# Grouping the split-array matmuls of a fused attention and mixture-of-experts kernel into two bursts a pass

## The chip, the cores and the metric

The kernel runs on one core of one Trainium2 chip, as one program. The metric is the device time of one execution in microseconds (us). Before the change it is 1570.88 us, the median of three runs (1569.62 to 1571.24).

## What is computed

`x` is 64 sequences of 128 tokens by 256, `ctx` 64 by 128 by 192, all float32. In the reference, cut to what matters:

```python
q = (layernorm(x) @ w_q) ; k = ctx @ w_k ; v = ctx @ w_v        # 16 heads of 64
attn = softmax(q k^T / 8) ; x = x + (attn v) @ w_o + b_o         # per sequence
h = layernorm(x)
g = top 2 of softmax(h @ gate) over 8 experts, renormalised
x = x + sum_e g_e * (relu(h @ W1[e] + b1[e]) @ W2[e] + b2[e])     # 256 -> 512 -> 256
```

## The kernel before

The first part, some 1,090 of the 1,568 us, is the attention: 32 passes over pairs of sequences (256 tokens), written as one loop body that each engine runs in its own order (`body(it)` of TensorE, VectorE, ScalarE, GpSimd and the DMA queue of SyncE), with the passes -1, 0, 1 and 31 unrolled. The second part multiplies the tokens, sorted by expert, in tiles of 256.

Each pass has eight slots, n = 0 to 7. What the slots hold is written out by hand:

- Projections go into PSUM banks (`product`, L1497). `q..` and `k..` are q and k of half of the heads, `v..` values, `o0`/`o1` the output projections of the two sequences, `f0` small counts for the routing. NEXT means that the product belongs to the next pass. To hold float32 precision a product is three matmuls of high and low halves (`three`, L1456).
- The attention itself works in units u0 to u7, each 4 heads of one sequence. TensorE multiplies the scores of two units side by side in the upper and lower 64 rows of its array (`scores`, L1469, L1477; 16 matmuls for two units). VectorE takes the row minimum (`lowest`, L985), ScalarE the exponentials and their sums (`exps`, L805), VectorE the reciprocals (`inverse`, L990), GpSimd scales (`norm`, L684), TensorE transposes (`transposes`, L1462), ScalarE copies the transposed bank (`copy_t`, L799), and TensorE multiplies with the values of two units side by side in two halves of the array's columns (`values`, L1482, L1492). ScalarE and VectorE then make the high and low half of the result (`hi_out`, L834, `low_out`, L1028).
- Slot n of TensorE holds: at even n the scores of units n and n+1, the transposes of unit n-2, products, and at odd n a group of values. So each pass has four groups of scores and four of values, and a group of values at the end of an odd slot stands right ahead of a group of scores.
- The statistics of the next pass's layernorm are taken on VectorE (`statistics`, `aggregate`), GpSimd makes the reciprocal root (`rstd_of`, slot 1), SyncE writes mean and root to DRAM and reads them back spread over all partitions (`ln_through`, L481: `ln_rows`, then `ln_all`), and GpSimd applies them to the transposed x (`normalise`, L695, slot 2, two operations L698 and L700). ScalarE and VectorE split that in halves (slot 4) for the products q of the next pass.
- `x_scores` (L1085, L1097) makes 16 dot products a pass on VectorE from `xin` and `gate_b`, both in SBUF, for the gate. They are spread over slots by `X_SCORES` (L1110).
- `send` (L673) scatters the pass's rows to the experts' lists with two indirect DMAs of GpSimd each, in slots 1 and 3. `rows_of` (L1079) on VectorE overwrites these rows and waits until all sends have landed. GpSimd also splits a piece of the experts' weights (L739) and adds the bias to the residual (L743).

Each engine works through its instructions in order, and a wait holds up all that stands behind it. There are eight PSUM banks: four for products, two for scores, one for transposes and one for values.

Of the kernel before, what the change touches and what calls it, by code (L numbers as in the profile page):

```python
# [73 lines left out]
def program(nc, x, x_t, ctx, w_all, w_ot, b_o, b_oc, gate, gate_t, w12, b1, b2, out):  # L74
# [50 lines left out]
    A_SLOTS_LAST = A_SLOTS[:4] + [[], [("v10", CUR)], [("v11", CUR)], [("f0", BOTH)]]  # L125
# [12 lines left out]
    OUT_SLOTS_LAST = OUT_SLOTS[:4] + [[], [], [("v10", CUR)], [("v11", CUR), ("f0", BOTH)]]  # L138
    A_EVENTS = [e for slot in A_SLOTS for e in slot]
    A_BANKS = 4  # L140

    BANK_OF = {"q10": 0, "k10": 1, "o0": 2, "k11": 3, "q11": 0, "o1": 1, "v10": 2, "v11": 3,
               "q00": 0, "q01": 1, "k00": 2, "k01": 3, "v00": 1, "f0": 0, "v01": 2}
# [9 lines left out]
    VALUES = {1: ("w3", PREV), 3: ("w0", CUR), 5: ("w1", CUR), 7: ("w2", CUR)}  # L153
    LAST = {0: ("w2", PREV), 2: ("w3", PREV), 4: ("w0", CUR), 6: ("w1", CUR)}

    ex = ExitStack()
    with ex:
# [3 lines left out]
        def signal(name, events):  # L161
# [3 lines left out]
                for n in ("a0", "a1", "a2", "a3", "s0", "s1", "t", "v")]  # L165
        bank_a, bank_s, bank_t, bank_v = psum[0:4], psum[4:6], psum[6], psum[7]
# [23 lines left out]
        with ExitStack() as a:  # L190
# [43 lines left out]
            kt = place("kt", 2, 2, CHUNKS // 2, P)  # L234
            place("not_used_1", WORK + 4 * HOME - taken_to[0])
# [3 lines left out]
            probt = place("probt", 2, 4, P)  # L239
# [67 lines left out]
            v_full, v_hi = (signal(name, list(VALUES.values())) for name in ("v_full", "v_hi"))  # L307
            v_lo = signal("v_lo", list(LAST.values()))
# [60 lines left out]
            def a_bank(name):  # L369
                return bank_a[BANK_OF[name]]  # L370

            def bank_before(it, name):

                same = [n for n, _ in A_EVENTS if BANK_OF[n] == BANK_OF[name]]
                if not isinstance(it, int):
                    k = same.index(name) - 1
                    return (it if k >= 0 else it - 1), same[k]
                order = [(j, n) for j in range(-1, PAIRS + 1) for n in a_full.present(j) if n in same]
                k = order.index((it, name)) - 1
                return order[k] if k >= 0 else (it, None)  # L380
# [61 lines left out]
            bank_at = {name: a_bank(name) for name in ("o0", "o1", "f0")}  # L442
            PLACES_AT = 5
            bank_h, bank_y = [bank_s, [bank_at["o0"], bank_at["o1"]]], [bank_t, bank_v]

            bank_first = a_bank("v11")
            assert len({id(bank) for bank in (bank_first, *bank_at.values())}) == A_BANKS

            def bank_x(j, u):

                return (bank_first, bank_at["f0"])[u % 2 if not isinstance(j, int) or j != PLACES_AT else 0]
# [170 lines left out]
            def _(pool):  # L622
# [60 lines left out]

                def norm(it, n):  # L684
# [1083 lines left out]
```

## Time and profile before

| | |
|---|---|
| median of three runs | 1570.88 us |
| profiled execution, its own time | 1569.98 us |
| span of the profile | 1568.2 us |
| granted TensorE clock, mean | 0.992 |
| busy share: TensorE, VectorE, ScalarE, GpSimd | 98%, 75%, 70%, 59% |
| one pass of attention | 33.73 us |

The span runs from the first to the last instruction, and the execution's own time has some 1.8 us around it. Engines are called PE (TensorE), DVE (VectorE), ACT (ScalarE), POOL (GpSimd) and SP (SyncE). Durations of neighbouring instructions on an engine overlap a little: an instruction's step is from its start to the start of the next one.

### The profile page before, as it was taken

Reading aid. Unit: us, or ns where it says so; the run is one execution under the profiler, and the core shown is the slowest. Engines: PE = TensorE matmul, PEld = TensorE weight load, DVE = VectorE, ACT = ScalarE, POOL = GpSimd, SP = SyncE. Lnnn points to the kernel's source line nnn. Section 1 sums busy time; section 2 is a strip of 40 time slices with the busy share of each in tenths; the row PEclk is TensorE's granted clock in tenths of the full one; section 3 lists DMA queues with packets and bytes.
Section 4 is the critical chain, followed back from the end, with each engine's and each line's share of the span. In section 5 each row is a group of like instructions: output and inputs, shape, how many; then the busy total and the mean of one; then the engine's idle time right before and its main releaser. Section 6 shows DMA issues by size and latency. Waiting matters only on the chain.

```text
span 1568.2 us, 45542 instructions
## 1 busy us (share of the span) xinstructions
PE 1542.6 (98%) x14030; PEld 1444.0 (92%) x14031; DVE 1179.0 (75%) x3734; ACT 1096.3 (70%) x3357; POOL 921.8 (59%) x1008
## 2 busy tenths in 40 slices
PE   8999999999999999999999999999999999999997
PEld 7999999999899999899999899988899999999996
DVE  4787777777787777787777777777788777777775
ACT  5777777677777677776777776767667667767764
POOL 3455656665665666665666565665365555555556
PEclk9999999999999999999999999999999999999999
DMA  6633222233222232222232222231799655555554
GB/s 214 162 92 94 74 74 83 88 105 94 74 74 81 87 108 89 79 74 81 81 114 83 85 74 78 83 99 64 253 250 239 126 85 89 85 86 89 85 85 61
DMA packets 123276, 161.65 MB, mean 103 GB/s; under 512 B 18208, under 2 KB 101280, under 8 KB 122976
## 3 DMA queue, kind: packets, MB, share of 16 engines
q1 hardware_dynamic: 77776, 105.59, 22.3%
q0 software_dynamic: 26816, 37.32, 13.7%
q10 hardware_dynamic: 18640, 18.19, 4.4%
q8 instruction: 23, 0.38, 0.1%
q14 instruction: 21, 0.17, 0.0%
HBM read 93.61 MB, written 67.44 MB: 103 GB/s over the span
## 4 chain that ended last, share of the span: by engine, by line
issue 42%; POOL 26%; DVE 8%; PE 8%; DMA 8%; DVEq 3%; ACT 2%; POOLq 2%; ACTq 1%; SPq 0%
DMA out<-stage_room,number 8%; POOL lists L680 7%; PE bank_a L1459 4%; DVE hid L1387 3%; POOL prob L687 3%; POOL xraw L698 3%; DVE stage_room L1404 3%; POOL stage_room L743 2%; POOL stage_room L739 2%; POOL xraw L700 2%; POOL mean_var L666 1%; DVEq L1399 1%; POOL rstd L666 1%; DVEq L1378 1%; POOL shifted L663 1%
## 5 line engine op out<-in xcount | busy, mean ns | idle before, releaser
L687 POOL TENSOR_TENSOR prob<-prob,inv 128x512 f32<-128x512 f32 x256 | 276.9, 1082 | 397.7 <-DVE inv L992 397.1
L809 ACT ACTIVATE prob<-bank_s,low 128x128 f32<-128x128 f32 x1024 | 362.5, 377 | 57.3 <-DVE low L987 57.2
L987 DVE TENSOR_REDUCE low<-bank_s 128x4 f32<-128x512 f32 x256 | 175.6, 686 | 121.2 <-PE bank_s L1477 121.1
L767 POOL DMA_INDIRECT out<-stage_room,number x142 | 230.4, 1622 | 54.1 <-issue 54.1
L802 ACT ACTIVATE probt<-bank_t 128x512 f32<-128x512 f32 x256 | 153.3, 599 | 109.0 <-PE bank_t L1466 109.0
L809 ACT ACTIVATION_READ_ACCUMULATOR prob<-bank_s,low 128x1 f32 x1024 | 222.0, 217 | 0.0
L1097 DVE SCALAR_TENSOR_TENSOR stage_room<-xin,wo_t 128x256 f32<-128x256 f32 x480 | 201.2, 476 | 0.0
L921 ACT ACTIVATE hidt_h<-hid 128x512 fp32r<-128x512 f32 x142 | 89.7, 632 | 129.6 <-DVE hid L1387 127.8
L837 ACT ACTIVATE ot_h<-bank_v 128x512 fp32r<-128x512 f32 x128 | 77.4, 604 | 140.8 <-PE bank_v L1492 140.7
L1466 PE MATMUL bank_t<-ident,prob 128*128 128x128 f32 x1024 | 161.8, 281 | 4.4 <-POOL prob L687 3.5
L1459 PE MATMUL bank_a<-xt_l,wq_h 128*128 128x256 f32 x512 | 151.2, 295 | 3.0 <-DVE xt_l L1067 3.0
L1477 PE MATMUL bank_s<-kt,qt 64*128 64x128 f32 x2048 | 149.7, 286 | 2.8 <-ACT prob L809 2.8
L680 POOL DMA_INDIRECT lists<-rows,slot x128 | 129.1, 1009 | 33.8 <-issue 33.6
L1477 PEld LDWEIGHTS bank_s<-kt,qt 64*128 64x128 f32 x2048 | 125.2, 188 | 25.1 <-issue 25.1
L1459 PE MATMUL bank_a<-wo_l,ot_h 128*128 128x264 f32 x496 | 146.3, 295 | 0.0
L1459 PE MATMUL bank_a<-xt_h,wq_l 128*128 128x256 f32 x512 | 145.9, 285 | 0.0
L1459 PE MATMUL bank_a<-xt_h,wq_h 128*128 128x256 f32 x512 | 145.8, 285 | 0.0
L1492 PE MATMUL bank_v<-probt,vv 128*64 128x128 f32 x2048 | 141.2, 280 | 0.8 <-issue 0.4
L1459 PE MATMUL bank_a<-wo_h,ot_l 128*128 128x264 f32 x496 | 141.2, 285 | 0.0
L1459 PE MATMUL bank_a<-wo_h,ot_h 128*128 128x264 f32 x496 | 140.8, 284 | 0.0
L901 ACT ACTIVATE wst<-homes 128x2048 fp32r x71 | 136.3, 1920 | 2.1 <-issue 2.1
L1466 PEld LDWEIGHTS bank_t<-ident,prob 128*128 128x128 f32 x1024 | 114.3, 141 | 25.1 <-POOL prob L687 5.8
(235 smaller groups left out, 4778.6 us busy)
## 6 DMA issues: line engine op xcount, KB each, us to landing
stage_room<-lists ACTq DMA_DIRECT2D x67, 265.0 KB, 2.9
halves<-stage_room SPq DMA_DIRECT2D x32, 512.0 KB
homes<-halves SPq DMA_DIRECT2D x16, 1024.0 KB, 6.8
xin<-in_x SPq DMA_DIRECT2D x32, 256.0 KB, 2.8
xraw<-in_x_t SPq DMA_DIRECT2D x32, 256.0 KB, 2.9
stage_room<-in_x SPq DMA_DIRECT2D x32, 256.0 KB, 3.1
stage_room<-in_w SPq DMA_DIRECT2D x32, 256.0 KB, 4.0
out<-stage_room SPq DMA_DIRECT2D x32, 256.0 KB, 2.2
```

What stands on the lines that cost most here:

```text
L680: pool.indirect_dma_start(lists, bass.IndirectOffsetOnAxis(ap=slot[:, b, k:k + 1], axis=0), rows[:, b, :], None).then_inc(sent, 16)
L687: pool.tensor_tensor(prob[:, n % 4, :, :], prob[:, n % 4, :, :], wide(inv[:, n % 4, :], P), ALU.mult).then_inc(s_norm.sem, 1)
L767: pool.indirect_dma_start(out, bass.IndirectOffsetOnAxis(ap=number[:, u, b:b + 1], axis=0), ysum[:, u, b, :], None, compute_op=ALU.add).th ...
L802: act.activation(probt[:, n % 2, :, :], bank_t[:, :].rearrange("p (h q) -> p h q", h=4), ACT.Copy).then_inc(t_copy.sem, 1)
L809: e = act.activation(prob[:, n % 4, h, :], bank_s[n % 2][:, h * P:(h + 1) * P], ACT.Exp, bias=low[:, n % 4, h:h + 1], scale=-1.0, accum_ou ...
L901: act.activation(wst[u % 2][:, :, :, :], homes[:, bass.ds(e, 2 * DC * H)].rearrange("p (c s h) -> p c s h", c=DC, s=2), ACT.Copy)
L987: dve.tensor_reduce(low[:, n % 4, :], bank_s[n % 2][:, :].rearrange("p (h k) -> p h k", h=4), AX.X, ALU.min).then_inc(s_low.sem, 1)
L1097: last = dve.scalar_tensor_tensor(junk[:, k % 11, :], xin[:, b, :], 1.0, gate_b[:, e, :], ALU.mult, ALU.mult, accum_out=x_two[:, b, e:e + 1])
L1459: last = pe.matmul(dst, stat[s], move[r], start=start and m == 0, stop=stop and m == 2)
L1466: last = pe.transpose(bank_t[:, h * P:(h + 1) * P], prob[:, n % 4, h, :], ident[:, :])
L1477: last = pe.matmul(bank_s[side][:, c * P:(c + 1) * P], qt[part, g, c, b * P:(b + 1) * P], kt[part, g, b, c, :], start=True, stop=True, ski ...
L1492: last = pe.matmul(bank_v[side, h * P:(h + 1) * P], vv[:, g, b, head * HEAD:(head + 1) * HEAD], probt[:, unit, h, :], start=True, stop=Tru ...
```

## The change

TensorE's scores and values are gathered. In slot 2 it does the values w2 and w3 of the pass before, and the scores of units 2 to 5. In slot 6 it does the values w0 and w1, the scores of units 6 and 7, and those of units 0 and 1 of the next pass. The scores get four banks, and the single bank of values is given up: products and values share a table of banks (`OCCUPANTS`), in which each waits until the one ahead of it in its row has been read. Three of the four banks of scores hold products as well. The products change slots. As the values v10 and v11 are now computed ahead of the last use of their predecessors, they go to a new buffer `v_new`, from which GpSimd carries them over (`new_values`, two operations of 128x512 a pass, in slot 2). On GpSimd `rstd_of` moves to slot 0, `normalise` moves ahead of the scaling of unit 2, and the sends are in slots 2 and 3. The 16 `x_scores` are split 8, 3 and 5 over slots 2, 4 and 5.

```diff
     A_SLOTS = [
-        [("q10", CUR), ("k10", CUR)],
+        [("k11", CUR), ("v10", CUR)],
+        [("v11", CUR)],
         [("o0", PREV)],
-        [("k11", CUR), ("q11", CUR)],
         [("o1", FROM0)],
-        [("v10", CUR), ("v11", CUR)],
         [("q00", NEXT), ("q01", NEXT)],
         [("k00", NEXT), ("k01", NEXT)],
-        [("v00", NEXT), ("f0", BOTH), ("v01", NEXT)],
+        [("v00", NEXT), ("v01", NEXT), ("q10", NEXT)],
+        [("k10", NEXT), ("f0", BOTH), ("q11", NEXT)],
     ]
     OUT_SLOTS = [
-        [("v01", NEXT)],
-        [],
-        [("o0", PREV)],
-        [("o1", FROM0)],
+        [("f0", BOTH)],
         [("v10", CUR), ("v11", CUR)],
         [],
+        [("o0", PREV), ("o1", FROM0)],
         [],
-        [("v00", NEXT), ("f0", BOTH)],
+        [],
+        [],
+        [("v00", NEXT), ("v01", NEXT)],
     ]
+    OCCUPANTS = [
+        [("w2", PREV), ("o1", FROM0), ("w0", CUR), ("v01", NEXT), ("q11", NEXT)],
+        [("v10", CUR), ("w3", PREV), ("q00", NEXT), ("w1", CUR), ("q10", NEXT)],
+        [("v11", CUR), ("o0", PREV), ("k00", NEXT), ("v00", NEXT), ("f0", BOTH)],
+        [("u4", CUR), ("u0", NEXT)],
+        [("u5", CUR), ("u1", NEXT)],
+        [("u2", CUR), ("q01", NEXT), ("u6", CUR), ("k10", NEXT)],
+        [("k11", CUR), ("u3", CUR), ("k01", NEXT), ("u7", CUR)],
+    ]
-    VALUES = {1: ("w3", PREV), 3: ("w0", CUR), 5: ("w1", CUR), 7: ("w2", CUR)}
-    LAST = {0: ("w2", PREV), 2: ("w3", PREV), 4: ("w0", CUR), 6: ("w1", CUR)}
+    BURSTS = {2: [("w2", PREV), ("w3", PREV)], 6: [("w0", CUR), ("w1", CUR)]}
...
# GpSimd
+                def new_values(it):
+                    for b in range(2):
+                        wait(pool, a_done, it, f"v1{b}")
+                        if has(it, PREV):
+                            wait(pool, v_full, it, f"w{2 + b}")
+                        pool.tensor_tensor(vv[:, 1, b, :].rearrange("p (k d) -> p k d", k=2),
+                                           v_new[:, b, :].rearrange("p (k d) -> p k d", k=2), pad[:, :, 0:D],
+                                           ALU.add).then_inc(v_copy.sem, 1)
...
-                        if n == 1 and has(it, NEXT):
+                        if n == 0 and has(it, NEXT):
                             rstd_of(it, 0)
...
+                        if n == 2 and has(it, NEXT) and not (isinstance(it, int) and it < 0):
+                            normalise(it)
+                        if n == 2 and has(it, CUR):
+                            new_values(it)
                         if has(it, CUR):
                             norm(it, n)
-                        if n == 2 and has(it, NEXT) and not (isinstance(it, int) and it < 0):
-                            normalise(it)
-                        if n in (1, 3) and has(it - 1, PREV):
-                            send(it - 1, n // 2)
+                        if n in (2, 3) and has(it - 1, PREV):
+                            send(it - 1, n - 2)
# ScalarE: hi_out of a burst comes first in slots 2 and 6, the halves of x and ctx move from slot 4 to 3
+                        for name, o in BURSTS.get(n, []):
+                            if has(it, o):
+                                hi_out(it, name)
                         late, of = LATE[n]
                         if has(it, of):
                             copy_t(it, late, (n - 2) % 8)
                         if n == 6 and has(it, PREV):
                             numerators(it, x1[:, :, D:])
-                        if n == 4 and has(it, NEXT):
+                        if n == 3 and has(it, NEXT):
...
# VectorE
-                X_SCORES = {1: [(0, 8)], 2: [(8, 3), (11, 3)], 5: [(14, 2)]}
+                X_SCORES = {2: [(0, 8)], 4: [(8, 3)], 5: [(11, 5)]}
...
+                        name, of = NEAR[n]
+                        if n in (2, 6) and has(it, of):
+                            inverse(it, name, n - 1)
+                        for name, o in BURSTS.get(n, []):
+                            if has(it, o):
+                                low_out(it, name)
                         if has(it, CUR):
                             lowest(it, n)
...
+                        if n not in (0, 2, 6) and has(it, of):
+                            inverse(it, name, n - 1)
...
+                        if n == 0 and has(it, NEXT):
+                            dve.wait_ge(x_in, (it + 2) * 16)
+                            statistics(0, xin)
...
                         for name, of in slots[n][1:]:
                             outcome(it, made_in, name, of)
+                        if n == 7 and has(it, CUR):
+                            inverse(it + 1, "u7", 7)
...
                         if n == 0 and has(it, NEXT):
-                            dve.wait_ge(x_in, (it + 2) * 16)
-                            statistics(0, xin)
+                            aggregate(it, 0)
...
# TensorE
-                        if n % 2 == 0 and has(it, CUR):
-                            scores(it, n)
+                        for name, o in BURSTS.get(n, []):
+                            if has(it, o):
+                                values(it, name)
+                        if n == 2 and has(it, CUR):
+                            scores(it, it, 2)
+                            scores(it, it, 4)
+                        if n == 6 and has(it, CUR):
+                            scores(it, it, 6)
+                        if n == 6 and has(it, NEXT):
+                            scores(it, it + 1, 0)
                         if has(it, of):
                             transposes(it, late, (n - 2) % 8)
...
-                        if n in VALUES and has(it, VALUES[n][1]):
-                            values(it, VALUES[n][0], n)
```

## Rows read from the trace of the kernel before

**Rows 1.** Windows view, one pass: us, then busy us and count by engine, clock, DMA.
```profile
504.05:537.78 33.73, 33.73 (x322) 30.78 (x321) 25.97 (x93) 24.20 (x89) 21.12 (x24) 1.00 0.28 86
```

**Rows 2.** Timeline of PE in that pass: start us, us, engine, line, operands.
```profile
509.29 0.60 PE L1466 MATMUL bank_t<-ident,prob 128*128 128x128 f32 x4
...
512.52 0.28 PE L1459 MATMUL bank_a<-wo_h,ot_h 128*128 128x264 f32 x1
512.73 1.09 PE L1492 MATMUL bank_v<-probt,vv 128*64 128x128 f32 x16
513.76 1.16 PE L1477 MATMUL bank_s<-kt,qt 64*128 64x128 f32 x16
514.85 0.66 PE L1466 MATMUL bank_t<-ident,prob 128*128 128x128 f32 x4
...
517.66 0.60 PE L1466 MATMUL bank_t<-ident,prob 128*128 128x128 f32 x4
...
521.05 1.09 PE L1492 MATMUL bank_v<-probt,vv 128*64 128x128 f32 x16
...
523.17 0.66 PE L1466 MATMUL bank_t<-ident,prob 128*128 128x128 f32 x4
...
526.05 0.60 PE L1466 MATMUL bank_t<-ident,prob 128*128 128x128 f32 x4
```

**Rows 3.** Timeline of ACT in that pass.
```profile
513.87 0.60 ACT L837 ACTIVATE ot_h<-bank_v 128x512 fp32r<-128x512 f32 x1 [1.55 <-PE bank_v L1492]
515.54 0.60 ACT L802 ACTIVATE probt<-bank_t 128x512 f32<-128x512 f32 x1 [1.07 <-PE bank_t L1466]
```

**Rows 4.** The page's groups: the exponentials, four to a unit.
```profile
L809 ACT ACTIVATE prob<-bank_s,low 128x128 f32<-128x128 f32 x1024 | 362.5, 377 | 57.3 <-DVE low L987 57.2
```

**Rows 5.** Timeline of DVE in that pass.
```profile
514.95 0.69 DVE L987 TENSOR_REDUCE low<-bank_s 128x4 f32<-128x512 f32 x1 [0.67 <-PE bank_s L1477]
...
525.05 0.17 DVE L1121 COPY g_turn<-g_exp 128x2 f32<-128x2 f32 x1 [1.01 <-ACT g_exp L830]
...
526.27 0.69 DVE L1034 TENSOR_TENSOR ot_l<-bank_v,ot_h 128x512 fp32r<-128x512 f32 x1
...
527.74 1.05 DVE L1145 TENSOR_TENSOR rows<-g_sel,g_inv 128x16 f32<-128x16 f32 x1
...
529.32 0.16 DVE L1013 TENSOR_TENSOR p_pos<-bank_a,run 128x16 f32<-128x16 f32 x1
...
530.62 0.17 DVE L992 RECIPROCAL inv<-total 128x4 f32<-128x4 f32 x1
...
533.11 0.74 DVE L1039 BATCH_NORM_STATS2 stats<-xin 128x6 f32<-128x256 f32 x2
```

**Rows 6.** Timeline of POOL in that pass.
```profile
507.12 1.04 POOL L687 TENSOR_TENSOR prob<-prob,inv 128x512 f32<-128x512 f32 x1 [3.80 <-DVE inv L992]
...
511.04 1.06 POOL L687 TENSOR_TENSOR prob<-prob,inv 128x512 f32<-128x512 f32 x1
512.04 1.54 POOL L698 TENSOR_TENSOR xraw<-xraw,ln_all 128x512 f32<-128x512 f32 x1
...
531.87 1.31 POOL L743 TENSOR_TENSOR stage_room<-stage_room,bo 128x512 f32<-128x512 f32 x1
534.60 1.26 POOL L687 TENSOR_TENSOR prob<-prob,inv 128x512 f32<-128x512 f32 x1 [1.42 <-DVE inv L992]
```

**Rows 7.** Timeline of DVE: dot products beside that last row of POOL, and after.
```profile
534.90 1.26 DVE L1097 SCALAR_TENSOR_TENSOR stage_room<-xin,wo_t 128x256 f32<-128x256 f32 x1
...
536.43 0.42 DVE L1097 SCALAR_TENSOR_TENSOR stage_room<-xin,wo_t 128x256 f32<-128x256 f32 x1
...
536.77 0.42 DVE L1097 SCALAR_TENSOR_TENSOR stage_room<-xin,wo_t 128x256 f32<-128x256 f32 x1
```

**Rows 8.** View of one line, L486 (`ln_rows`), all passes: issue to landing.
```profile
DMA to landing us min/median/max: 1.4/1.4/3.2
```

**Rows 9.** The same view of L489 (`ln_all`).
```profile
DMA to landing us min/median/max: 3.3/4.3/5.2
```

More of the change, by code:

```diff
@@ L367, in by_products, with place_of, a_bank, held_before @@
                 return isinstance(it, int) and it < 1
[L369 to L374, printed above, removed]
+            def place_of(name):
+                return next(k for k, held in enumerate(OCCUPANTS) if name in [n for n, _ in held])
+            def a_bank(it, name):
+                return bank_s[2] if isinstance(it, int) and (it, name) == (PAIRS, "f0") else psum[place_of(name)]
+            def held_before(it, name):
+                held = OCCUPANTS[place_of(name)]
                 if not isinstance(it, int):
-                    k = same.index(name) - 1
-                    return (it if k >= 0 else it - 1), same[k]
-                order = [(j, n) for j in range(-1, PAIRS + 1) for n in a_full.present(j) if n in same]
+                    k = [n for n, _ in held].index(name) - 1
+                    return (it if k >= 0 else it - 1), held[k][0]
+                order = [(j, n) for j in range(-1, PAIRS + 1) for n, of in held if has(j, of)]
                 k = order.index((it, name)) - 1
@@ L859, in body @@
                                 hi_part(it, name)
-                        if n == 4 and has(it, NEXT):
+                        if n == 3 and has(it, NEXT):
                             wait(act, a_full, it, "v11")
@@ L1163, in outcome @@
                         slots_of(made_in)
-                    if name == "f0" and has(it, CUR):
-                        inverse(it + 1, "u7", 7)
                 def body(it):
@@ L1467, in transposes, with released, scores @@
                     last.then_inc(t_full.sem, 1)
-                def scores(it, n):
-                    g, b = n // 4, (n % 4) // 2
-                    wait(pe, a_hi, it if g else it - 1, "q11" if g else "k01")
-                    wait(pe, s_exp, it, f"u{n + 1}", 2)
+                def released(it, name):
+                    kind = name[0]
+                    if kind == "w":
+                        wait(pe, v_lo, it, name)
+                    elif kind == "u":
+                        wait(pe, s_exp, it + 1 if name in ("u0", "u1") else it, name)
+                    else:
+                        wait(pe, a_hi if kind in "qk" else a_done, it, name)
+                def scores(body_it, it, n):
+                    g, b = n // 4, (n % 4) // 2
+                    if n in (0, 4):
+                        wait(pe, a_hi, it if g else it - 1, "k11" if g else "k01")
+                    for unit in (n, n + 1):
+                        earlier, of = held_before(body_it, f"u{unit}")
+                        if of is not None:
+                            released(earlier, of)
                     for c in range(CHUNKS // 2):
@@ L1476, in scores @@
                             part = slice(side * HEAD, (side + 1) * HEAD)
-                            last = pe.matmul(bank_s[side][:, c * P:(c + 1) * P], qt[part, g, c, b * P:(b + 1) * P],
+                            last = pe.matmul(bank_s[(n + side) % 4][:, c * P:(c + 1) * P], qt[part, g, c, b * P:(b + 1) * P],
                                              kt[part, g, b, c, :], start=True, stop=True, skip_group_check=True)
@@ L1480, in scores, with values @@
                                 last.then_inc(s_full.sem, 1)
-                def values(it, name, n):
+                def values(it, name):
                     g, b = int(name[1]) // 2, int(name[1]) % 2
-                    wait(pe, a_done, it if name == "w2" else it - 1, f"v{g}{b}")
-                    wait(pe, t_copy, it, LATE[n][0])
-                    wait(pe, v_lo, it, LAST[n - 1][0])
+                    wait_for = {"w0": (it, "u1"), "w1": (it, "u3"), "w2": (it - 1, "u5"), "w3": (it, "u7")}[name]
+                    if g:
+                        wait(pe, v_copy, it - 1, f"c1{b}")
+                    else:
+                        wait(pe, a_done, it - 1, f"v0{b}")
+                    wait(pe, t_copy, *wait_for)
+                    earlier, of = held_before(it, name)
+                    if of is not None:
+                        released(earlier, of)
+                    dst = a_bank(it, name)
                     for head in range(HALF):
@@ L1608, in body @@
                             keep_busy(8)
-                        if n in VALUES and has(it, VALUES[n][1]):
-                            values(it, VALUES[n][0], n)
+                        if isinstance(it, int) and (it, n) == (PAIRS - 1, 7):
+                            values(PAIRS, "w2")
                 def keep_busy(many):
@@ L1632, in gate_means @@
                     for c in range(DC):
-                        last = pe.matmul(bank_v[:, 0:E], prob[:, 0, 0, :], gate_sb[:, c, :], start=c == 0, stop=c == DC - 1,
+                        last = pe.matmul(bank_t[:, 0:E], prob[:, 0, 0, :], gate_sb[:, c, :], start=c == 0, stop=c == DC - 1,
                                          skip_group_check=True)
@@ L1657, in turn_x @@
                         if j < 2:
-                            wait(pe, a_done, PAIRS - 1, "v11" if j == 0 else "f0")
+                            wait(pe, s_exp, PAIRS - 1, "u7")
                         elif j == PLACES_AT + 2:
```

101 lines of the change are left out of this document (47 added, 54 removed).

## The prediction

> **What bounds the kernel now.** I read the windows view first. In one pass TensorE is busy all of its 33.73 us at the full granted clock, while VectorE has 26, ScalarE 24 and GpSimd 21 us of work [rows 1]. So a pass lasts as long as TensorE's own instruction stream, and anything saved there comes off the time until another chain becomes longer. Second, the timeline of TensorE shows what that stream loses. Twenty-four product matmuls run from behind the four transposes at 509.29 to 512.52, a step of about 0.12. From the end of that step (512.64) to the next transposes at 514.85 the split-array work takes 2.21 us [rows 2]. The values row spans 1.09 for sixteen matmuls of which each lasts 0.27, so the eight pairs follow at about 0.11; sixteen pairs (values and scores) are 1.76 us of work [rows 2]. The other 0.45 us is lost where full-array, column-split, row-split and full-array work meet: between the last product matmul and the values, in front of the scores, and in front of the transposes. Third, the timelines of the other engines give the steps with which I walk through the new order. The reader is to see that these engines have slack in sum, but that this says nothing of a chain that has to be finished between two points of TensorE's stream.
>
> **What is removed.** Four bursts (values, then scores) become two, each with two value groups and four units of scores. The work inside stays: 64 matmuls of either kind a pass. Two meetings of forms are saved per pass, 2 x 0.45 = 0.9 us [rows 2], and over the run 128 bursts become 65, so 63 x 0.45 = 28 us. Pass length would be 32.83 us if no other wait appeared. The additional PSUM banks, the bank table and the changed slots issue no instruction, so they cost only through waits. The second part of the kernel keeps its order.
>
> **TensorE's new stream,** from rows 2. Transposes with one o behind them take 3.35 us to the next transposes (509.29 to 512.64), with two v 2.8 (514.85 to 517.66), with two q 3.3 (517.66 to 521.05 less the 0.1 of the burst), with two k 2.9 (523.17 to 526.05). Transposes alone are 0.44, so v, k and q are about 1.17, 1.2 and 1.43 each. In a burst that starts at 0, scores start at 1.03 + 0.88 = 1.9 and the transposes at 1.9 + 1.09 + 0.88 = 3.9. I call the two bursts B6 and B2 by their slots.
>
> **From B6 to B2.** Behind B6: transposes of u4 at 3.9, v00, v01, q10, transposes of u5 at 8.1, k10, f0, q11, transposes of u6 at 11.3, k11, v10, transposes of u7 at 14.1, v11, B2 at 15.8. One wait arises there. The bank of q11 is v01's, and VectorE empties it last in a row of gate_top (1.2, from 525.05 to 526.27 [rows 5]), a minimum (0.6), the gate weights and two copies (1.6 from 527.74 to 529.32 plus one more copy of 0.6 [rows 5]), which can start only at about 5.8, when ScalarE has copied u4's transposes (0.69 behind them, 514.85 to 515.54 [rows 2, 3]) and made the numerators. It is done at 9.9 where q11 is due at 9.9. If VectorE arrives later, from `rows_of`, which now waits for sends that are issued later, it is up to 0.7 late. I take 0.4, so B2 is at 16.2.
>
> **The layernorm chain of the next pass.** ScalarE reads q10's bank at 8.3, copies u5's transposes and has the exponentials of u7 at 10.7 (two copies of 0.6 that overlap by 0.1, and four exponentials of 0.377 that overlap [rows 3, 4]). VectorE then has in order the reciprocal, the minimum of u0 (0.6), the statistics (0.7), the routing of f0 (1.3, 529.32 to 530.62) and only then `aggregate` (0.2) [rows 5]. That ends at 13.6, or 14.1, as two operands of the routing lie in SBUF and GpSimd's L743 (1.31 [rows 6]) runs there; I take 14.1. The root is about 1.0 (an estimate: two tiny operations, held to be no longer than one scaling of 1.04 [rows 6]). Mean and root land in DRAM 1.4 us after issue [rows 8] and spread over the partitions 4.3 after theirs [rows 9]. `normalise` can start at 14.1 + 1.0 + 1.5 + 4.3 = 20.9, which is B2 + 4.7.
>
> **Slot 2, where I expect the loss.** GpSimd now has normalise (2 x 1.54 = 3.1 [rows 6]), the two copies of new_values, the scaling of u2 (1.0), then a send, in this order. A copy is not in the trace; it has two streaming SBUF operands of 128x512 as L743 (1.31), while the scaling with its short second operand takes 1.04 [rows 6]. So the two cost 2.1 to 2.6; I take 2.6, as L743's form is theirs. VectorE has, from B2: the low half of w3 at 2.0 + 0.6 to 3.25 (ScalarE starts 1.14 behind the start of a group, 512.73 to 513.87 [rows 2, 3]), the minimum of u2 (seen 1.19 behind the scores, 513.76 to 514.95 [rows 2, 5]) until 3.85, then eight dot products of 0.35 (536.43 to 536.77 [rows 7]), then the minimum and the reciprocal of u3 and u2. GpSimd's scaling of u2 needs that reciprocal.
>
> Dot products and GpSimd's work exclude each other. The one issued at 534.90, while GpSimd's scaling ran from 534.60 to 535.86, took 1.26 instead of 0.42, and the scaling itself took 1.26 instead of 1.04 [rows 6, 7]. The dot products of slot 2 run from B2 + 3.85, and normalise arrives at B2 + 4.7. Whoever goes first, the work adds up: 2.8 + 3.1 + 2.6 = 8.5, to B2 + 12.35. If dot products are last, the minimum, the reciprocal and the scaling follow (0.6 + 0.3 + 1.05 + 0.1) and u2 can be transposed at B2 + 14.4. If GpSimd is last, only the scaling follows, and it is 13.5. TensorE wants it at 3.9 + 3.4 + 3.35 = 10.65. The wait is 2.85 to 3.75, or from 2.35 with copies of 1.04; I take 3.3, between the two orders.
>
> By the Trainium skill (SBUF — State Buffer, Who interferes with whom) a VectorE instruction with two SBUF inputs is held for the whole of a GpSimd instruction that reads SBUF, and the other way round. The row of the scaling agrees with 1.26 us, and no row has normalise beside dot products. By that rule the loss is the one just worked out; without it, it is that of the first rival below.
>
> **Slot 3.** A scaling that is followed by a send starts 3.92 before the next scaling (507.12 to 511.04 [rows 6]). TensorE needs 3.3 between the transposes of u2 and u3. So u3 is 0.6 late again, up to 1.1 if the low half of the context on VectorE holds its scaling up; I take 0.7. Before, normalise stood between these scalings with time to spare, as the pass had its longest TensorE stretches there. The last reads of u4 to u7 stay ahead of their transposes by 1 us and more.
>
> **The sum.** Per pass -0.9 + 0.4 + 3.3 + 0.7 = +3.5. Dot products are in the passes 1 to 30, so 30 x 3.5 = 105, less 1.4 for the three bursts merged elsewhere: +103.6. The profiled execution took 1569.98 us (span 1568.2 and 1.8 around it), 0.9 below the median of the runs. 1569.98 + 103.6 + 0.9 gives 1674 us. The ends of this case: -0.9 + 0 + 2.35 + 0.6 = +2.05, 1631 us, and -0.9 + 0.7 + 3.75 + 1.1 = +4.65, 1709 us. Chance 0.59.
>
> **Rivals.** First, only the order on GpSimd tells, and the dot products find gaps. Then u2 is ready at B2 + 4.7 + 3.1 + 2.6 + 1.25 = 11.65, a wait of 1.0, and u3 0.6, q11 0.2: +0.9 a pass, 1597 us. With the shortest landing (3.3) and copies of 1.04 the wait at u2 is gone and the pass gains 0.3 to 0.8, so 1548 to 1615 with all ends. For it: VectorE has 7.7 us of slack a pass [rows 1], and dot products elsewhere in that pass cost 0.42. Against it: eight in a row cannot find gaps in 5.7 us of GpSimd work without any. Chance 0.21.
>
> Second, the other side: TensorE stays the bound and the change gives all it removes, 63 x 0.45 = 28 us, 1543 us. This needs u2 scaled by B2 + 10.65. It speaks for it that GpSimd is busy only 21 of 33.7 us [rows 1] and that its chain did not hold TensorE before. It decides from an `aggregate` that ends 3.3 us earlier than I have it, or 1.0 earlier if dot products and GpSimd did not exclude each other. Chance 0.16.
>
> Third, the chain is longer than I have it and runs round: late sends hold `rows_of`, this the dot products, these the next load of x, and the pass takes more than 38.5 us, over 1712. Chance 0.04. A variant that cuts across all is that the 0.45 belongs to each group and not to the change of form, so that merging saves nothing; it would put each case 28 us higher and lies inside the range.
>
> The Trainium skill (TensorEngine Tiling (Array Packing), its note that mode switching requires a drain) says that changing the tiling mode, not the tile, empties the array. By it a merged group pays once, as I count it. Rows 2 show the gap at each meeting, and none has two groups of one form in a row, so the trace leaves this variant open.
>
> **Range and chances.** From 1560 to 1712 us; left out are the second rival, the third and the far end of the first. The likeliest case alone spans 1631 to 1709. A measurement of this kernel tells 0.2% (3 us) from no change. Faster: 0.16 and a quarter of the first rival, 0.21. Same: 0.04, where the first rival crosses zero. Slower: the rest, 0.75.
>
> **What would show it.** In the changed profile: 65 bursts, scores of four units in a row without a gap after the second; a pass near 37.3 us; TensorE idle in front of u2's transposes by about 3 us and in front of u3's by 0.7, released by GpSimd's scaling; dot products of 1.3 to 1.8 us in slot 2; normalise starting nearly 5 us behind B2. Wrong would be: a pass near 32.8 with no idle time in front of transposes, normalise started before B2 + 4, or dot products that keep 0.42 beside it.

## The result and the profile after

The changed kernel takes 1686.66 us (median of four runs, 1684.48 to 1688.80), beside 1570.81 before: a ratio of 1.074, 95% interval 1.0727 to 1.0753. Forecast was 1674. It is slower by 115.9 us where 103.6 were worked out.

The page of the changed kernel, busy time by engine, and under it its windows view of one pass, of the stretch from B6 to B2, and of a stretch behind u2's transposes (columns: us, busy us by engine, granted clock of full speed, DMA):

```profile
PE 1567.2 (93%) x14030; PEld 1485.0 (88%) x14031; DVE 1335.8 (79%) x3734; ACT 1104.6 (65%) x3357; POOL 1004.0 (60%) x1072
```

```profile
542.87:580.21 37.34, 34.75 (x321) 32.36 (x320) 31.39 (x93) 24.35 (x90) 23.65 (x27) 0.95 0.25 78
542.87:559.05 16.18, 16.03 (x149) 14.40 (x148) 13.23 (x50) 11.88 (x42) 8.81 (x12) 1.00 0.17 50
...
573.00:577.00 4.00, 4.00 (x22) 4.00 (x23) 3.91 (x14) 2.56 (x11) 3.51 (x4) 0.58 0.65 189
```

The pass shown takes 37.34 us in place of 33.73 [rows 1]; over 28 passes the mean is 37.23. TensorE runs the same 14,030 matmuls and is no longer busy all the time. From B6 to B2 it is busy almost throughout. VectorE is busy 31.4 us in place of 26, with the same number of instructions: the additional 5.4 us are instructions that take longer. And the granted clock is 0.58 in a stretch behind the wait.

TensorE's timeline, changed kernel:

```profile
542.87 1.97 PE L1533 MATMUL bank_r<-probt,vv 128*64 128x128 f32 x32
544.76 2.06 PE L1513 MATMUL bank_s<-kt,qt 64*128 64x128 f32 x32
546.75 0.66 PE L1489 MATMUL bank_t<-ident,prob 128*128 128x128 f32 x4
...
559.05 1.97 PE L1533 MATMUL bank_r<-probt,vv 128*64 128x128 f32 x32
...
562.93 0.66 PE L1489 MATMUL bank_t<-ident,prob 128*128 128x128 f32 x4
...
566.34 0.60 PE L1489 MATMUL bank_t<-ident,prob 128*128 128x128 f32 x4
...
572.27 0.66 PE L1489 MATMUL bank_t<-ident,prob 128*128 128x128 f32 x4 [2.44 <-POOL prob L701]
...
573.33 0.42 PE L1482 MATMUL bank_r<-xt_h,wq_h 128*128 128x256 f32 x1
573.54 0.41 PE L1482 MATMUL bank_r<-xt_l,wq_h 128*128 128x256 f32 x1
...
576.58 0.28 PE L1482 MATMUL bank_s<-xt_l,wq_h 128*128 128x256 f32 x1
576.70 0.28 PE L1482 MATMUL bank_s<-xt_h,wq_l 128*128 128x256 f32 x1
...
577.29 0.60 PE L1489 MATMUL bank_t<-ident,prob 128*128 128x128 f32 x4
```

The merged burst works as meant: values 1.89 us, scores 1.99, transposes 3.88 behind its start, where two bursts of before took two times 2.12 to the same point (512.73 to 514.85 [rows 2]). That is 0.36 less; 0.09 ahead of the values and 0.06 behind the transposes are saved as well, 0.51 in all. Then the transposes of u2 stand at B2 + 13.2 (572.27 less 559.05) where they were due 3.33 behind those of u1 at 566.34, thus at B2 + 10.6. The wait is 2.6 us and its releaser is GpSimd's scaling. Behind it the product matmuls are 0.21 apart in place of 0.12 until 576.3, so from u2's transposes to u3's it is 5.0 us in place of 3.3.

The wait and the clock are not tied as firmly as this pass suggests. In each of the passes 1 to 30 TensorE is idle for 2.43 to 2.52 us in front of u2's transposes, but the granted clock fell to its lower level in 24 of them, for 3.4 us each time, and stayed up in six. One of the six, TensorE's timeline:

```profile
461.10 0.66 PE L1489 MATMUL bank_t<-ident,prob 128*128 128x128 f32 x4 [2.45 <-POOL prob L701]
465.28 0.66 PE L1489 MATMUL bank_t<-ident,prob 128*128 128x128 f32 x4 [0.50 <-POOL prob L701]
```

Here u3 follows u2 after 4.18 us and waits for GpSimd's scaling, which stands behind the send. Such passes take 36.4 to 36.7 us, but for one at the end of the loop. So the slower clock costs some 0.7 us in the passes that have it.

GpSimd and VectorE in the same stretch, changed kernel, timelines:

```profile
563.87 1.55 POOL L712 TENSOR_TENSOR xraw<-xraw,ln_all 128x512 f32<-128x512 f32 x1 [2.55 <-DMA ln_all<-ln_rows]
565.50 1.61 POOL L714 TENSOR_TENSOR xraw<-xraw,ln_all 128x512 f32<-128x512 f32 x1
567.06 2.71 POOL L694 TENSOR_TENSOR vv<-v_new,pad 128x512 f32<-128x512 f32 x2
571.17 1.04 POOL L701 TENSOR_TENSOR prob<-prob,inv 128x512 f32<-128x512 f32 x1 [1.40 <-DVE inv L1011]
...
572.98 1.05 POOL L685 DMA_INDIRECT lists<-rows,slot  x1 [0.17 <-issue]
...
575.33 1.06 POOL L701 TENSOR_TENSOR prob<-prob,inv 128x512 f32<-128x512 f32 x1
```

```profile
562.90 0.41 DVE L1118 SCALAR_TENSOR_TENSOR stage_room<-xin,wo_t 128x256 f32<-128x256 f32 x1
...
563.93 1.77 DVE L1118 SCALAR_TENSOR_TENSOR stage_room<-xin,wo_t 128x256 f32<-128x256 f32 x1
...
565.64 1.75 DVE L1118 SCALAR_TENSOR_TENSOR stage_room<-xin,wo_t 128x256 f32<-128x256 f32 x1
...
567.32 1.40 DVE L1118 SCALAR_TENSOR_TENSOR stage_room<-xin,wo_t 128x256 f32<-128x256 f32 x1
...
568.65 1.40 DVE L1118 SCALAR_TENSOR_TENSOR stage_room<-xin,wo_t 128x256 f32<-128x256 f32 x1
...
569.99 0.41 DVE L1118 SCALAR_TENSOR_TENSOR stage_room<-xin,wo_t 128x256 f32<-128x256 f32 x1
...
570.33 0.68 DVE L1006 TENSOR_REDUCE low<-bank_s 128x4 f32<-128x512 f32 x1
570.94 0.16 DVE L1011 RECIPROCAL inv<-total 128x4 f32<-128x4 f32 x1
```

Three dot products run freely in 0.35 each. Then each of the four GpSimd operations holds one dot product until it ends, the last one is free again, and only then come the minimum of u3 and the reciprocal (570.94) for which GpSimd itself has been idle 1.40 us. From the start of the first dot product (562.90) to that of the minimum behind the last (570.33) it is 7.4 us, where eight dot products of 0.35 and GpSimd's operations at their undisturbed lengths (3.1, and 2.35 by a run below) add up to 8.25. So the sum is an upper bound here: a held dot product still ends 0.2 to 0.3 us after the next GpSimd operation has started.

### The profile page after: what moved, and what is told of

Its sections match the earlier page's. It is cut to its first block, busy times and chain, and to the rows that moved or that the text cites. A ratio compares the mean times of both kernels' runs of the same rounds, so it can differ in the third digit from the quotient of the medians.

```text
span 1687.0 us, 45817 instructions
## 1 busy us (share of the span) xinstructions
PE 1567.2 (93%) x14030; PEld 1485.0 (88%) x14031; DVE 1335.8 (79%) x3734; ACT 1104.6 (65%) x3357; POOL 1004.0 (60%) x1072
## 4 chain that ended last, share of the span: by engine, by line
issue 43%; POOL 29%; DVE 9%; PE 6%; DMA 5%; DVEq 3%; POOLq 2%; ACT 2%; ACTq 1%
POOL prob L701 6%; POOL lists L685 6%; POOL vv L694 5%; DMA out<-stage_room,number 4%; POOL xraw L712 3%; DVE hid L1410 3%; DVE stage_room L1427 3%; POOL stage_room L759 2%; POOL stage_room L755 2%; PE bank_r L1482 2%; DVEq L1422 1%; POOL out L783 1%; DVEq L1401 1%; POOLq L777 1%; POOLq L71 1%
## 5 line engine op out<-in xcount | busy, mean ns | idle before, releaser
L1118 DVE SCALAR_TENSOR_TENSOR stage_room<-xin,wo_t 128x256 f32<-128x256 f32 x480 | 334.0, 755 | 0.0
L1482 PE MATMUL bank_r<-wo_l,ot_h 128*128 128x264 f32 x496 | 145.8, 294 | 0.0
L1482 PE MATMUL bank_r<-wo_h,ot_l 128*128 128x264 f32 x496 | 140.7, 284 | 0.0
L1482 PE MATMUL bank_r<-wo_h,ot_h 128*128 128x264 f32 x496 | 140.3, 283 | 0.0
L1513 PE MATMUL bank_s<-kt,qt 64*128 64x128 f32 x2048 | 132.7, 280 | 0.7 <-ACT kt L838 0.7
L1482 PE MATMUL bank_r<-xt_l,wq_h 128*128 128x256 f32 x384 | 125.2, 326 | 6.8 <-DVE xt_l L1088 1.9
L1533 PE MATMUL bank_r<-probt,vv 128*64 128x128 f32 x2048 | 127.0, 277 | 0.9 <-issue 0.9
L1533 PEld LDWEIGHTS bank_r<-probt,vv 128*64 128x64 f32 x2048 | 111.2, 137 | 16.6 <-issue 12.5
L1482 PE MATMUL bank_r<-xt_h,wq_h 128*128 128x256 f32 x384 | 119.4, 311 | 0.0
L1482 PE MATMUL bank_r<-xt_h,wq_l 128*128 128x256 f32 x384 | 119.0, 310 | 0.0
```

The costliest lines, as they stand in the source:

```text
L1118: last = dve.scalar_tensor_tensor(junk[:, k % 11, :], xin[:, b, :], 1.0, gate_b[:, e, :], ALU.mult, ALU.mult, accum_out=x_two[:, b, e:e + 1])
L1482: last = pe.matmul(dst, stat[s], move[r], start=start and m == 0, stop=stop and m == 2)
L1513: last = pe.matmul(bank_s[(n + side) % 4][:, c * P:(c + 1) * P], qt[part, g, c, b * P:(b + 1) * P], kt[part, g, b, c, :], start=True, stop ...
L1533: last = pe.matmul(dst[side, h * P:(h + 1) * P], vv[:, g, b, head * HEAD:(head + 1) * HEAD], probt[:, 2 * b + unit, h, :], start=True, sto ...
```

## The experiments

Times are medians, and each ratio is to the kernel before on the same chip (1570.87, 1569.21 or 1569.70 us). "Behind the burst" is behind B2.

**The dot products in slot 1.** Theory A of the expectations is the exclusion of the prediction, theory B its first rival.

```diff
-                X_SCORES = {2: [(0, 8)], 4: [(8, 3)], 5: [(11, 5)]}
+                X_SCORES = {1: [(0, 8)], 4: [(8, 3)], 5: [(11, 5)]}
```

> The eight dot products of slot 2 move to slot 1 of VectorE, ahead of the burst; nothing else changes. Theory A (dot products and GpSimd's normalise and copies exclude each other, and the reciprocal of u2 stands behind the dot products): the reciprocal is then ready 7 us behind the burst, GpSimd works through normalise (3.1) and the copies (2.7) undisturbed from 4.8, and u2's transposes stand at 11.8 behind the burst in place of 13.2, a wait of 1.2 in place of 2.6. Send sets u3's 0.6 later than TensorE wants. A pass of 34.8 us if the granted clock then stays full, 36 if it still falls; 1610 to 1645 us. Theory B (normalise simply starts too late, the dot products find gaps): u2's transposes stay at 13.2, 1687 us.

Measured 1614.21 us, ratio 1.028 (1.0262 to 1.0294). TensorE's two waits, timeline of this kernel, whose B2 is at 559.54, and its windows row of the pass:

```profile
571.29 0.66 PE L1489 MATMUL bank_t<-ident,prob 128*128 128x128 f32 x4 [0.97 <-POOL prob L701]
575.17 0.66 PE L1489 MATMUL bank_t<-ident,prob 128*128 128x128 f32 x4 [0.35 <-POOL prob L701]
```

```profile
543.34:578.14 34.80, 33.33 (x322) 30.86 (x321) 27.61 (x92) 24.67 (x90) 23.26 (x27) 1.00 0.27 84
```

The pass is 34.80 and u2's transposes stand at 11.75, as theory A has it. No dot product of slot 1 is held, and the granted clock stays full behind the wait of 1 us, in all of the passes 1 to 30. One edited line gives back 72 us of the 116. Theory B falls.

**The copies in slot 5.** `new_values(it)` on GpSimd behind the work of slot 5.

```diff
-                        if n == 2 and has(it, CUR):
-                            new_values(it)
...
+                        if n == 5 and has(it, CUR):
+                            new_values(it)
```

> Only the two copies of the values move on GpSimd, from slot 2 ahead of the scaling of u2 to slot 5, where it stands idle for 3 us. Theory A: the excluded work in slot 2 is 2.7 us shorter, the dot products end at 9.8 behind the burst, u2's transposes stand at 11.9 in place of 13.2: a wait of 1.3, a pass of 34.9 to 36, 1612 to 1645 us. Theory B: normalise ends at 8.1 and the scaling follows at once, so u2's transposes are at 10.6, no wait, a pass near 33.1 and 1560 us.

Measured 1657.13 us, ratio 1.055 (1.0535 to 1.0567). u2's transposes are at 11.25 behind the burst (591.87 beside a B2 of 580.61), halfway between theory A's 11.9 and theory B's 10.6. TensorE still waits 0.48 us for u2's scaling, and with the dot products gone as well, in the next run, it doesn't. So they do hold this chain, but by less than their full sum. Also, B6 to B2 is now 17.7 us in place of 16.2: a new wait, which neither theory had. The next run shows what it is.

**Both moved,** the two edits above together.

> Dot products in slot 1 and copies in slot 5 together. Theory A and B both: the scaling of u2 starts at 8.0 behind the burst, its transposes do not wait, u3's neither (13.0 against 13.9 wanted). A pass of 33.0 us, the clock stays full, 1555 us, some 1% below the kernel before the change. If it stays above 1600, a third cause holds the pass, such as the late sends that hold rows_of and the next load of x.

Measured 1622.13 us, ratio 1.033 (1.0317 to 1.0346): 67 us more than expected, and 8 us more than with the first edit alone. Each single edit helps, and both together are worse than the better of them. GpSimd's and VectorE's timelines in slots 5 and 6, and the waits view of the pass:

```profile
587.11 2.35 POOL L694 TENSOR_TENSOR vv<-v_new,pad 128x512 f32<-128x512 f32 x2
```

```profile
587.71 0.63 DVE L1142 COPY g_turn<-g_exp 128x2 f32<-128x2 f32 x1
...
588.51 0.97 DVE L1147 SCALAR_TENSOR_TENSOR g_sum<-g_best 128x2 f32<-128x2 f32 x1
```

```profile
PE bank_r L1617 <- DVE vv L1020: 1.0, 1, 1.0
```

u2 doesn't wait any more. The copies now stand beside gate_top: a copy of two elements a partition takes 0.63 in place of 0.17 [rows 5], and an operation on two elements 0.97, where it takes 0.16 in the kernel before. VectorE empties v00's bank later, and f0 (L1617), which takes over that bank, waits 1.0 us for it. u3 also waits 0.5: its reciprocal stands behind the minimum of u4, which stands behind o1.

**The copies on ScalarE.** With the dot products in slot 1, ScalarE makes the copies behind `hi_out` in slot 2, and GpSimd has no `new_values`.

```diff
+                        act.activation(vv[:, 1, b, :], v_new[:, b, :], ACT.Copy).then_inc(v_copy.sem, 1)
...
                                hi_out(it, name)
+                        if n == 2 and has(it, CUR):
+                            new_values(it)
```

> Dot products in slot 1, and the two copies of the values on ScalarE behind hi_out in slot 2, which shares no port with VectorE. Theory A: u2 does not wait and neither GpSimd nor VectorE is held in slots 5 and 6, where the copies held gate_top by 1.3 us. u3 still waits 0.5 for its reciprocal behind the minimum of u4. A pass of 33.6 us, 1578 us. If the copies in slot 5 were not what held gate_top, 1622 us as with both moved.

Measured 1582.25 us, ratio 1.0086 (1.0071 to 1.0102), a pass of 33.76. With no copy on GpSimd, B6 to B2 is back to 16.2 us (17.5 with both moved), so it was the copies that held gate_top.

**And the reciprocal of u3 taken in slot 3.**

```diff
-                        if n not in (0, 2, 6) and has(it, of):
+                        if n not in (0, 2, 4, 6) and has(it, of):
                             inverse(it, name, n - 1)
...
                             low_of_tokens(it)
+                        if n == 3 and has(it, CUR):
+                            inverse(it, "u3", 3)
```

> As the last, and the reciprocal of u3 taken in slot 3 behind the low half of x, ahead of o1. u3 is scaled in time, a pass of 33.0 us (33.73 before the change, less 0.9 for the merged bursts, plus 0.2), 1559 us, 0.7% below the kernel before. If merging saved nothing, a pass of 33.9 and 1585 us.

Measured 1562.40 us, ratio 0.9965 (0.9952 to 0.9979), a pass of 33.06: u3's transposes follow u2's after 3.31 us in place of 3.98.

**And the gate weights behind v00 and v01,** except in the last pass.

```diff
-                        if n == 7 and has(it, PREV):
+                        last_pass = isinstance(it, int) and it == PAIRS - 1
+                        if n == 7 and last_pass:
                             gate_weights(it)
...
                         for name, of in slots[n][1:]:
                             outcome(it, made_in, name, of)
+                        if n == 7 and has(it, PREV) and not last_pass:
+                            gate_weights(it)
```

> The best version so far with the gate weights on VectorE behind the two copies v00 and v01 in slot 7, except in the last pass: q11 and f0 then find their banks empty, the last wait of 0.2 us a pass goes, 32.85 us a pass, 1556 us. If the wait of q11 is covered by something else, 1562 us.

Measured 1552.17 us, ratio 0.9898 (0.9883 to 0.9913): 1.0% faster than the kernel before, with the merged bursts in it. Windows view, one pass of it:

```profile
514.60:547.34 32.74, 32.74 (x321) 30.78 (x320) 24.32 (x93) 25.39 (x93) 21.06 (x25) 1.00 0.28 88
```

TensorE is busy all of 32.74 us. Against 33.73 [rows 1], with all waits gone, the two merged bursts of a pass are worth 0.99, thus 0.50 each, which agrees with the 0.51 counted in the burst itself. This settles the variant that merging saves nothing: it falls.

**A dose of dot products.** Eleven in slot 2.

```diff
+                X_SCORES = {2: [(0, 8), (8, 3)], 5: [(11, 5)]}
```

> A dose: eleven dot products in slot 2 in place of eight, the three of slot 4 moved there. Theory A: each adds its 0.35 to the excluded work, u2's transposes are 1.05 later (14.3 behind the burst), 30 passes by 1.05: 1718 us. Theory B: GpSimd does not feel them, but the reciprocal of u2 is still ahead of need, 1687 us.

Measured 1730.60 us, ratio 1.102 (1.1004 to 1.1037). u2's transposes are at 14.26 behind the burst, as theory A has it, where 13.2 is the changed kernel's. The time moved by 44 and not 31 us: passes are 38.2 to 39.4. The dose accounts for 1.05 a pass. The rest goes along with the clock, which now fell in each of the passes 1 to 29, and in every third, those of 39.3 us and more, stayed low for 6.8 us in place of 3.4.

**An earlier layernorm.** `aggregate` straight behind the statistics and the minimum of u0, from pass 2 on.

```diff
+                        early = n == 0 and has(it, NEXT) and (not isinstance(it, int) or it > 1)
+                        if early:
+                            dve.wait_ge(x_in, (it + 2) * 16)
+                            statistics(0, xin)
+                            wait(dve, ln1_step, it, "bn1_1")
+                            dve.wait_ge(ln_out, it * 16)
                         if has(it, CUR):
                             lowest(it, n)
+                        if early:
+                            aggregate(it, 0)
...
```

> The changed kernel, with aggregate straight behind the minimum of u0, ahead of the routing of f0, so that normalise can start about 1.2 us earlier. Theory A (the excluded work adds up): dot products and GpSimd's work only interleave earlier, their end moves by 0 to 0.3 us, 1678 to 1687 us. Theory B (normalise starts too late): the whole 1.2 us come off, 1650 us.

Measured 1680.91 us, ratio 1.0716 (1.0699 to 1.0732). GpSimd's timeline, whose B2 is at 593.04:

```profile
596.89 1.83 POOL L712 TENSOR_TENSOR xraw<-xraw,ln_all 128x512 f32<-128x512 f32 x1 [1.58 <-DMA ln_all<-ln_rows]
...
605.17 1.04 POOL L701 TENSOR_TENSOR prob<-prob,inv 128x512 f32<-128x512 f32 x1 [2.09 <-DVE inv L1011]
```

normalise starts 3.85 behind the burst, 1.0 earlier than in the changed kernel, and the scaling of u2 starts at 12.13, where it is 12.12 in the changed kernel (571.17 less 559.05). Four dot products are held here as there; only fewer of the free ones come ahead of them (one in place of three), and more behind. So when normalise starts counts for next to nothing. The run gained 6 us all the same: in the mean of the passes u2's transposes come 0.15 us earlier, and the clock fell in 21 of the passes 1 to 30 in place of 24.

**Filling the wait, to keep the clock.** In front of u2's transposes TensorE multiplies the identity by itself, 20 times.

```diff
+                    wait(pe, t_copy, it, name, 1)
+                    if name == "u2" and (not isinstance(it, int) or 1 <= it <= PAIRS - 2):
+                        for _ in range(20):
+                            pe.matmul(bank_t[:, 0:P], ident[:, :], ident[:, :], start=True, stop=True,
+                                      skip_group_check=True)
                     wait(pe, s_norm, it - 1 if n >= 6 else it, name)
-                    wait(pe, t_copy, it, name, 1)
```

> The changed kernel, with 20 matmuls of the identity by itself (2.2 us, into the empty bank of transposes) in the 2.6 us in which TensorE waits for u2. Theory clock: the 1.7 us that lie between the transposes of u2 and u3 beyond the 3.3 of before come from the granted clock that falls to its lower level behind the wait; with TensorE busy it stays, the distance is then set by the send (3.95 to 4.2), 0.8 to 1 us a pass less, 1657 to 1663 us. Rival: TensorE reads xt late or beside the DMA traffic there, and the filler changes nothing or costs: 1687 us or more.

Measured 1697.21 us, ratio 1.082 (1.0804 to 1.0837). The clock stayed (mean 0.992 in place of 0.966) and u3's transposes followed u2's in 3.3 us in place of 5.0. But each filling matmul took twice what I had counted, so together they ended 1.9 us behind the moment at which u2's transposes start in the changed kernel. As u2 was late itself, the time cannot say what the clock costs. With half as many:

```diff
-                        for _ in range(20):
+                        for _ in range(10):
```

> As the filler before, with 10 matmuls in place of 20: one took 0.22 us and not the 0.11 that I had counted, so 20 took 4.45 us and made u2 late themselves. Ten take 2.2 us of the wait of 2.6. Theory clock: u2's transposes stay at 13.2 behind the burst, the clock stays at its upper level, and u3's follow after 3.95 to 4.2 (set by the send) in place of 5.0: a pass of 36.3 to 36.6 us and 1655 to 1663 us. Rival: 5.0 stays, 1687 us.

Measured 1670.97 us, ratio 1.0647 (1.063 to 1.0663), 16 us less than the changed kernel. Timeline of TensorE and windows row of this pass, whose B2 is at 587.90:

```profile
598.51 2.39 PE L1489 MATMUL bank_t<-ident 128*128 128x128 f32 x20
601.14 0.66 PE L1493 MATMUL bank_t<-ident,prob 128*128 128x128 f32 x4 [0.23 <-POOL prob L701]
...
605.32 0.66 PE L1493 MATMUL bank_t<-ident,prob 128*128 128x128 f32 x4 [0.51 <-POOL prob L701]
```

```profile
571.71:608.30 36.59, 35.70 (x341) 33.13 (x340) 31.24 (x92) 24.43 (x92) 23.62 (x27) 1.00 0.24 79
```

The profile shows each filling matmul as two (x20 for ten). u2 stands at 13.2 as in the changed kernel, the matmuls behind it are at full clock, and u3 follows after 4.2, released by the scaling behind the send, as in the six passes of the changed kernel whose clock stayed up. It is the wait that the prediction put at 0.7, and that the slow clock had covered. So of the 1.7 us by which u3 is late, 0.9 are the send's and 0.8 the clock's. The pass shown is 0.75 us shorter than the changed kernel's, the mean of 28 passes 0.56 (36.68 beside 37.23), as the clock had not fallen in each of them. The time came out 8 us above the expected range.

**Values and scores taken in turns** within each burst, on the kernel of 1562.40 us: values, scores, values, scores.

```diff
+                        if groups:
+                            values(it, groups[0][0])
+                        if n == 2 and has(it, CUR):
+                            scores(it, it, 2)
...
+                        if groups:
+                            values(it, groups[1][0])
+                        if n == 2 and has(it, CUR):
+                            scores(it, it, 4)
...
```

> The best version so far (1562 us) with each burst in the order values, scores, values, scores in place of values, values, scores, scores: the same bursts against the full-array work, but three meetings of column-split and row-split work in place of one. If a change of form costs as such (0.2 us between values and scores in the trace), 2 x 0.4 a pass: 33.85 us a pass, 1587 us. Rival (what a burst costs belongs to leaving and re-entering the full array, or to each group whatever stands ahead): 1562 us.

Measured 1596.82 us, ratio 1.0171 (1.0155 to 1.0186). Timeline of TensorE, a B2 and, first, a B6:

```profile
297.32 1.09 PE L1533 MATMUL bank_r<-probt,vv 128*64 128x128 f32 x16
298.88 1.16 PE L1513 MATMUL bank_s<-kt,qt 64*128 64x128 f32 x16 [0.47 <-ACT kt L827]
...
314.39 1.09 PE L1533 MATMUL bank_r<-probt,vv 128*64 128x128 f32 x16
315.41 1.16 PE L1513 MATMUL bank_s<-kt,qt 64*128 64x128 f32 x16
316.50 1.09 PE L1533 MATMUL bank_r<-probt,vv 128*64 128x128 f32 x16
317.53 1.16 PE L1513 MATMUL bank_s<-kt,qt 64*128 64x128 f32 x16
318.62 0.65 PE L1489 MATMUL bank_t<-ident,prob 128*128 128x128 f32 x4
```

The B2 takes 4.23 us to the transposes in place of 3.88: two more meetings of forms, 0.17 each. In B6 the scores come 0.53 later, since they stand earlier in the burst and wait for ScalarE's copy of k01, whose bank u7 takes over. So 0.7 of the 1.2 us that a pass is longer (34.26 beside 33.06) belongs to the change of form, and 0.5 to that wait.

## Why the prediction was right

**What bounds, and what is saved.** 128 bursts became 65, as forecast. The saving was taken as 0.45 us for each merged burst and is 0.50, by the pass of 32.74 us without waits. The sum left out the 0.06 right behind the transposes that follow a burst. By the Trainium skill (TensorEngine Tiling (Array Packing), Key Properties) a change of tiling mode drains the array, and a change of tile alone doesn't. The traces agree with it: a merged group paid once, and two more changes between the forms inside a burst cost 0.17 each.

**B6 to B2.** 15.8 plus 0.4 was forecast, 16.18 measured, and 15.88 in the kernel without this wait. The wait at q11 is thus 0.3 us, and gone when the gate weights stand behind the two copies.

**The layernorm chain.** normalise was put at B2 + 4.7 and started at 4.82. As the run with the earlier layernorm shows, this number mattered little.

**Slot 2.** The mechanism is shown by the held dot products of 1.40 to 1.77 us and by three runs: taking dot products out gives u2 at 11.75 where 11.8 was worked out, adding three gives 14.26 where 14.3 was, and an earlier normalise changes next to nothing. The size was off: the wait is 2.6 us in place of 3.3. The dot products did come last, the order for which the prediction had u2 at B2 + 14.4 and a wait of 3.75, and u2 came at 13.2. The shared work ended 1.1 earlier than the sum had it (B2 + 11.3 and not 12.35): two copies take 2.35 us undisturbed and not 2.6, and held dot products overlap a little with the next GpSimd operation. The value taken between the two orders hid a part of this error. The first rival falls as an account of the whole, but a part of it was right: with the dot products away, the order on GpSimd alone still leaves waits of 1.2 and 0.6 (it had 1.0 and 0.6), and that kernel is 43 us slower than the one before the change.

**Slot 3.** 0.7 was forecast for the send, and u3 is 1.7 late. Where the clock stays up, with ten filling matmuls and in six passes of the changed kernel, it is 0.9 behind the send alone. The rest is the granted clock, a cost that the prediction did not have at all.

**The sum.** Per pass +3.5 was forecast. From the first transposes of pass 1 to those of pass 29 the trace has 28 passes of 37.23 us mean against 33.73, thus +3.5. In the pass shown it is +3.6: -1.0 for bursts, +0.3 at q11, +2.6 at u2, and +1.7 between u2 and u3. That the total fits so closely is luck. 0.7 too much at u2, and 0.1 each for the bursts and at q11, made up for 0.8 of the clock, which the sum did not have, and for a send taken 0.2 too short.

The 12 us missed do not lie in these passes. Of the 118.8 us by which the span grew, 98 are in them, 11 ahead of them and 9 behind them, where the sum had 5.6 for both ends. (The medians of the runs are 2.9 us less apart than the two profiled spans.) The 11 us are there before pass 0 has its first transposes, which start at 42.0 us in place of 30.9. TensorE has done 48 more matmuls by then (214 in place of 166), as pass -1 now makes products that were made in pass 0. The prediction put this start at nothing. The second part of the kernel, behind the last transposes, takes the same time in both (459.8 and 459.7). The best version pays for the start too: its passes save 0.95 in the mean, 26.7 us in 28 of them, its first transposes are at 40.2, and its time falls by 17.5. No run was made on the ends. So it is shown where the 12 us lie, and only argued, from the counts, why.

**The second rival,** all waits hidden, was wrong for this kernel, but what it asked for could be had: other places for eight dot products, two copies and two small instructions turn +7.4% to -1.0%.

## What to carry to other kernels

When work is merged on the engine that bounds, the stretches between other engines' deadlines become unequal: walk each chain against its deadline, not against its engine's busy share. VectorE's dot products, which read two operands from SBUF, and GpSimd's operations nearly add up as if on one engine (7.4 us where their sum is 8.25), whoever starts first. So put them beside different things, or move the GpSimd work to ScalarE. Work that is moved one pass ahead may be paid for once in front of the loop (here the first transposes came 11 us later). A wait of TensorE can have a second price behind it, the clock (here behind 2.4 us of idle time in 24 of 30 passes), and that price can cover smaller waits.

## What was not expected of the hardware

- Behind 2.4 us of idle time the granted clock fell from its upper level (2.4 GHz) to its lower (1.2 GHz) in 24 of 30 passes, for 3.4 us each (0.58 mean from 573 to 577, matmul step 0.21 in place of 0.12), and in six it did not. With the copies in slot 5, idle times of 1.4 to 1.6 us were followed by the lower level in six passes and not in as many others. With the dot products in slot 1, TensorE was idle for 0.9 to 1.6 us in front of u2 in each pass, and the clock did not fall once in the passes 1 to 30.
- Exclusion reaches tiny instructions: a copy of 128x2 in SBUF took 0.63 and an operation of 128x2 with two SBUF operands 0.97 us beside a GpSimd copy, in place of 0.17 and 0.16.
- A float32 matmul of the identity took 0.22 to 0.24 us (2.39 us for ten) and shows as two records; a transpose of the same size took 0.11.
- A change between column-split and row-split matmuls costs 0.17 us, and leaving the full array for both and coming back 0.50, that change included.
